# An audio tower on one core: how normalised tokens, projections and residual sums are handed between VectorE and TensorE around the attention

## The reference, cut to what matters

```
h = x[:, None, :]                                  # 64 sequences of 4000 samples
for w, g, b, s in convs:                           # seven convolutions, 128 channels
    h = gelu(layernorm(conv1d(h, w, s), g, b))     # layernorm over the channels
h = layernorm(h, fln_g, fln_b) @ proj_w + proj_b   # 64 x 12 tokens of 192
h = h + landmark_attention(layernorm(h))           # 12 heads of 16, pseudo-inverse in 6 rounds
h = h + experts(layernorm(h))                      # 8 routed experts, one shared
```

## Time and profile before

| | |
|---|---|
| time, median of 3 runs | 875.67 us (874.26 to 878.14) |
| profiled execution: its time | 875.06 us |
| profiled execution: span from first to last instruction | 873.3 us |
| busy, TensorE's matmuls | 757.3 us, 87% of the span |
| busy, VectorE | 624.9 us, 72% |
| busy, ScalarE | 329.4 us, 38% |
| busy, GpSimd | 314.7 us, 36% |

### The profile page before, as it was taken

How to read it: one execution, slowest core, us unless ns; L and a number is a source line. 1 busy time by engine, 2 the same in 40 slices (tenths; PEclk the granted TensorE clock), 3 DMA queues, 4 the chain that set the end, 5 groups by cost and what they waited for, 6 DMA issues and landing times. The chain is left out here.

```text
span 873.3 us, 11965 instructions
## 1 busy us (share of the span) xinstructions
PE 757.3 (87%) x4308; PEld 578.2 (66%) x4308; DVE 624.9 (72%) x1373; ACT 329.4 (38%) x562; POOL 314.7 (36%) x365
## 2 busy tenths in 40 slices
PE   0099999999998999999899898787888887899997
PEld 0055565656565655665565678677888886899977
DVE  7965778786788675456556568998888888462387
ACT  0054473436643565453332124022333321245433
POOL 1332313133133123212000037457777885247301
PEclk9997987998899989997898899899999999989999
DMA  2430520024000600000000430000000000200000
GB/s 74 85 88 1 102 53 1 1 47 106 1 1 12 130 1 1 1 1 0 1 1 2 171 165 1 1 1 1 1 1 1 1 2 0 82 1 1 1 1 28
DMA packets 23424, 25.50 MB, mean 29 GB/s; under 512 B 17370, under 2 KB 21530, under 8 KB 22442
## 3 DMA queue, kind: packets, MB, share of 16 engines
q1 hardware_dynamic: 23096, 24.17, 11.1%
q10 hardware_dynamic: 270, 0.58, 0.3%
HBM read 21.05 MB, written 3.66 MB: 28 GB/s over the span
## 5 line engine op out<-in xcount | busy, mean ns | idle before, releaser
L521 POOL TENSOR_TENSOR diff<-h 128x400 f32<-128x400 f32 x112 | 98.4, 901 | 280.1 <-ACT h L661 169.2
L607 PEld LDWEIGHTS ps<-averager,sq 128*100 128x100 f32 (+2 forms) x1024 | 105.3, 174 | 35.6 <-ACT sq L656 20.2
L607 PE MATMUL ps<-averager,sq 128*100 128x1 f32 (+2 forms) x1024 | 102.6, 227 | 9.6 <-ACT sq L656 9.4
L567 PE MATMUL ps<-h,w 128*128 128x400 f32 x224 | 108.1, 610 | 1.9 <-ACT h L635 1.1
L760 DVE TENSOR_TENSOR h<-ps,shared 128x800 f32<-128x800 f32 x56 | 55.4, 989 | 65.5 <-PE ps L576 65.5
L656 ACT ACTIVATE sq<-h 128x800 f32<-128x800 f32 (+1 forms) x58 | 50.1, 864 | 118.2 <-DVE h L760 111.0
L1103 PE MATMUL pt<-for_pe,ident 128*128 128x156 f32 (+2 forms) x420 | 70.1, 328 | 24.8 <-DVE for_pe L1302 24.8
L576 PE MATMUL ps<-diff,w 128*128 128x400 f32 x224 | 91.5, 530 | 0.0
L795 DVE TENSOR_TENSOR h<-h,ps 128x400 f32<-128x400 f32 (+1 forms) x116 | 61.5, 560 | 33.4 <-PE ps L626 33.0
L1103 PEld LDWEIGHTS pt<-for_pe,ident 128*128 128x128 f32 x420 | 63.7, 204 | 30.1 <-DVE for_pe L1302 27.7
L635 ACT ACTIVATE h<-ps,lnp 128x800 f32<-128x800 f32 x64 | 63.7, 1013 | 39.5 <-PE ps L540 39.4
(11 more groups left out here) (302 smaller groups left out, 1357.5 us busy)
## 6 DMA issues: line engine op xcount, KB each, us to landing
late<-windows_dram SPq DMA_DIRECT2D x18, 375.0 KB, 8.1
gate_w<-in_gate_w SPq DMA_DIRECT2D x1, 3456.0 KB, 11.5
up_w<-in_up_w SPq DMA_DIRECT2D x1, 3456.0 KB, 19.0
windows_dram<-parts SPq DMA_DIRECT2D x9, 250.0 KB, 5.5
acts<-in_down_w SPq DMA_DIRECT2D x1, 1728.0 KB, 9.0
late<-windows_dram SPq DMA_DIRECT2D x18, 93.8 KB, 4.8
w<-in_w SPq DMA_DIRECT2D x1, 1024.0 KB, 6.0
xs<-in_x SPq DMA_DIRECT2D x4, 252.5 KB, 3.7
```

Source lines behind the costliest of these rows:

```text
L521: pool.tensor_tensor(to[:, rows, :], here[:, rows, :], behind[:, rows, :], ALU.subtract).then_inc(diff_ready, 1)
L567: pe.matmul(out[:, c, :, :], w[:, L.first_tap + 1, :], plane(l, s, p, 1, slice(c, L.pos, 2)), start=True, stop=False)
L607: mm = pe.matmul(var_ps[0:L.w, at:at + 1], sq[:, square_of[r, l, s, p // 2] % 2, p % 2, q * L.w:(q + 1) * L.w], averager[:, 0:1], start=Tr ...
```

## The change

`normalise` writes the variance plus EPS where the copy put it, so the copy is gone (in all three uses). With a semaphore given, each normalised tile adds one to it, and TensorE's transposes wait tile by tile (`tokens_normed`, `x_normed`); the two telling copies are gone. Scale and offset are applied in two instructions, four tiles (one PSUM bank) and two, as soon as those are turned, and the projection waits for each part. The two projections tell after each pair of tiles (`tiles_projected`), and the additions behind them wait pair by pair. The blocks of `stay_warm` keep their lengths and places.

```
@@ normalise: EPS goes straight into stats, the copy goes, tiles are told one by one @@
-def normalise(nc, steps, src, dst, stats, mv, y, t, u):
+def normalise(nc, steps, src, dst, stats, mv, y, t, u, normed=None):
...
-    steps.done(nc.vector.tensor_scalar(mv[:, :, 1], mv[:, :, 1], EPS, None, ALU.add))
-    steps.settle()
-
-    steps.done(nc.vector.tensor_copy(stats[:, :, 0], mv[:, :, 1]))
+    steps.done(nc.vector.tensor_scalar(stats[:, :, 0], mv[:, :, 1], EPS, None, ALU.add))
     steps.settle()
     rsqrt(nc, steps, stats[:, :, 0], y, t, u)
     for i in range(TT):
-        steps.done(nc.vector.tensor_scalar(dst[i], src[i], mv[:, i, 0:1], y[:, i:i + 1], ALU.subtract, ALU.mult))
+        tile = nc.vector.tensor_scalar(dst[i], src[i], mv[:, i, 0:1], y[:, i:i + 1], ALU.subtract, ALU.mult)
+        if normed is None:
+            steps.done(tile)
+        else:
+            tile.then_inc(normed, 1)
     steps.settle()
 
 
-def turn(pe, ps, src, ident, done):
+def turn(pe, ps, src, ident, done, normed):
 
     for k in range(KD):
         for t in range(TT):
+            pe.wait_ge(normed, t + 1)
             mm = pe.transpose(ps[0:96, k, t * P:(t + 1) * P], src[:, t, 96 * k:96 * k + 96], ident[:, :])
         mm.then_inc(done, 1)
...
@@ attention, TensorE @@
                 stay_warm(bank(3, 1), 14)
-                pe.wait_ge(to_pe, 1)
                 for t in range(TT):
-                    mm = pe.transpose(pt[:, 1, t * P:(t + 1) * P], norm6[:, t, :], ident[:, :])
-                mm.then_inc(turned, 1)
+                    pe.wait_ge(tokens_normed, t + 1)
+                    pe.transpose(pt[:, 1, t * P:(t + 1) * P], norm6[:, t, :], ident[:, :]).then_inc(tokens_turned, 1)
                 stay_warm(bank(3, 1), 4)
-                pe.wait_ge(to_pe, 2)
                 pe.wait_ge(a_in, 16 * LOADS)
                 for t in range(TT):
+                    pe.wait_ge(to_pe, 1 + (t >= FIRST_TILES))
                     mm = pe.matmul(pt[:, 2 + t // 4, (t % 4 // 2) * 512 + (t % 2) * D:(t % 4 // 2) * 512 + (t % 2) * D + D],
                                    norm6t[:, t * P:(t + 1) * P], proj_w[:, :], start=True, stop=True)
-                mm.then_inc(projected, 1)
+                    if t % 2:
+                        mm.then_inc(tiles_projected, 1)
                 stay_warm(bank(3, 1), 26)
+                turn(pe, pt, xhat, ident, half_turned, x_normed)
+                stay_warm(bank(3, 1), 4)
                 pe.wait_ge(to_pe, 3)
-                turn(pe, pt, xhat, ident, half_turned)
-                stay_warm(bank(3, 1), 4)
-                pe.wait_ge(to_pe, 4)
                 pe.wait_ge(half_copied, 1)
...
@@ attention, VectorE @@
-                normalise(nc, steps, [pt[:, 0, t * P:(t + 1) * P] for t in range(TT)], tile(norm6), *small)
-                nc.vector.tensor_copy(t6[:, :], y6[:, :]).then_inc(to_pe, 1)
-                dve.wait_ge(turned, 2)
-                nc.vector.tensor_scalar(norm6t[:, :], pt[:, 1, 0:TOK], lnp[:, 14:15], lnp[:, 15:16],
-                                        ALU.mult, ALU.add).then_inc(to_pe, 1)
-                dve.wait_ge(projected, 1)
+                normalise(nc, steps, [pt[:, 0, t * P:(t + 1) * P] for t in range(TT)], tile(norm6), *small, tokens_normed)
+                for first, end in ((0, FIRST_TILES), (FIRST_TILES, TT)):
+                    dve.wait_ge(tokens_turned, end)
+                    nc.vector.tensor_scalar(norm6t[:, first * P:end * P], pt[:, 1, first * P:end * P], lnp[:, 14:15], lnp[:, 15:16],
+                                            ALU.mult, ALU.add).then_inc(to_pe, 1)
                 dve.wait_ge(a_in, 16 * LOADS)
...
-                for out, bank in projected_tiles():
+                for c, (out, bank) in enumerate(projected_tiles()):
+                    dve.wait_ge(tiles_projected, c + 1)
                     steps.done(nc.vector.tensor_tensor(out, bank, proj_b[:, :].unsqueeze(1).broadcast_to([P, 2, D]), ALU.add))
                 steps.settle()
-                normalise(nc, steps, tile(hidden), tile(xhat), *small)
-                nc.vector.tensor_copy(t6[:, :], y6[:, :]).then_inc(to_pe, 1)
+                normalise(nc, steps, tile(hidden), tile(xhat), *small, x_normed)
                 dve.wait_ge(half_turned, 1)
...
-                dve.wait_ge(projected, 2)
-                for out, bank in projected_tiles():
+                for c, (out, bank) in enumerate(projected_tiles()):
+                    dve.wait_ge(tiles_projected, TT // 2 + c + 1)
                     steps.done(nc.vector.tensor_tensor(out, out, bank, ALU.add))
```

More of the change, by code:

```diff
@@ L83 @@
 PADS = LANDMARKS - SEQ
+FIRST_TILES = 512 // P
 PINV_ITERS = 6
@@ L899, in attention @@
     to_pe = sem("to_pe")
-    projected = sem("projected")
+    tokens_normed = sem("tokens_normed")
+    tokens_turned = sem("tokens_turned")
+    tiles_projected = sem("tiles_projected")
+    x_normed = sem("x_normed")
     qkv_ready = sem("qkv_ready")
@@ L1128, in _ @@
                 stay_warm(bank(3, 1), 5)
-                pe.wait_ge(to_pe, 5)
+                pe.wait_ge(to_pe, 4)
                 pe.wait_ge(heads_ready, 2)
@@ L1260, in _ @@
                 copies(applying, at_applying)
-                act.wait_ge(turned, 3)
+                act.wait_ge(turned, 2)
                 for half in range(2):
@@ L1411, in _ @@
                                         attn[:, :, :].rearrange("p i (h d) -> p i h d", d=DH), ALU.subtract).then_inc(out_lanes, 1)
-                dve.wait_ge(turned, 3)
+                dve.wait_ge(turned, 2)
                 steps.done(nc.vector.tensor_copy(*heads_turned(1, 0)))
                 nc.vector.tensor_copy(*heads_turned(1, 1)).then_inc(to_pe, 1)
-                dve.wait_ge(projected, 2)
-                for out, bank in projected_tiles():
+                for c, (out, bank) in enumerate(projected_tiles()):
+                    dve.wait_ge(tiles_projected, TT // 2 + c + 1)
                     steps.done(nc.vector.tensor_tensor(out, out, bank, ALU.add))
```

## The result

| | before | after |
|---|---|---|
| time, median of 9 runs | 876.23 us (871.83 to 880.56) | 870.73 us (867.46 to 873.62) |
| ratio of the runs, 95% interval | | 0.9938 (0.9913 to 0.9963) |
| profiled execution, span | 873.3 us | 869.6 us |

The change takes 0.6% off, 5.4 us of 876 by the ratio, with 3.2 to 7.6 us inside the interval. The forecast was 869.8 us (867.2 to 872.6).

What follows compares the result with a forecast made beforehand. The bound was taken to be the back-and-forth chain between TensorE and VectorE. Terms 3.16 + 1.07 + 0.93 + 0.75 = 5.91 us took 875.06 to 869.15 us; 0.61 us for the median gave 869.8 us (867.2 to 872.6).

Steps and rivals of the forecast that it cites:

- The chain: Attention's opening: TensorE and VectorE wait on each other in turn; the edits start q, k and v 3.16 us earlier.
- Short steps: Copy dropped in each `normalise`: 0.20 us each for the first two; the third, before the experts, hidden by TensorE's `stay_warm`.
- Tokens turned by tile: Opening: first projection starts 1.27 us earlier, including the first 0.20 us short step; bounds 0.9 and 1.8 us.
- Bias and residual additions: Behind both projections: with additions by pairs, two of three are hidden, saving 0.93 us at each place.
- `turn`: Second six transposes, tile by tile: ScalarE's copy begins 1.05 instead of 1.81 us after VectorE's last tile, saving 0.76 us.
- the cover: The `stay_warm` block of 52 records behind the first projection: ends 0.7 us before VectorE's last tile, taken as enough slack.
- Clock behind `turn`: At the first q, k, v tile: TensorE's fall to 1.2 GHz goes with the wait, saving 1.07 us; other bound nothing.
- slower: Rival, chance 0.04: the 52-record `stay_warm` block runs at 1.2 GHz and becomes the bound; 878.8 us.
- Clock at the experts' start: Experts' `stay_warm` block: without the fall to 1.2 GHz VectorE is the bound, saving 0.75 us; bounds 0 and 0.75.
- Clock terms absent: Rival, chance 0.26: TensorE's clock still falls, behind another gap or before q, k, v; 4.09 us saved, 871.6 us.
- A fall less elsewhere: Rival, chance 0.12: one clock fall fewer in the iteration, worth at most 1.68 us; 868.1 us.
- Tiles bring nothing: Rival, chance 0.06: covers or per-tile waits hold TensorE; only short steps and last additions' pairs count, 1.7 us; 874.0 us.

Runs made afterwards that it cites:

- e1_short_step: Kernel before with only the variance-plus-EPS copy removed in all three uses of `normalise`; first `stay_warm` block to q, k, v 21.35 us, 0.43 less.
- e8_further: Changed kernel plus statistics begun after four turned tiles, scale and offset in three instructions, shorter `stay_warm` before the projection; 867.59 us, ratio to kernel before 0.9940.
- e3_pairs: Kernel before with only projections telling and additions waiting by pairs of tiles; first `stay_warm` block to q, k, v 20.83 us, output projection to experts 5.27 us.
- e4_turn: Kernel before with only the second `normalise` and `turn` going tile by tile; first `stay_warm` block to q, k, v 21.01 us, 0.77 less.
- e9_long_block: Changed kernel with 32 instead of 26 `stay_warm` matmuls behind the first projection; first `stay_warm` block to q, k, v 19.29 us, 0.91 more.
- e2_tokens: Kernel before with only tokens turned tile by tile and scale and offset in two instructions; first `stay_warm` block to q, k, v 20.45 us, 1.33 less.
- e5: Kernel before with 35 instead of 26 `stay_warm` matmuls, filling the wait before `turn`; first `stay_warm` block to q, k, v 21.75 us, first tile 2.21 us.
- e7: Changed kernel with 27 more semaphore increments on matmuls that nobody waits for; q, k, v products 11.88 us, output projection 4.14 us, as without them.
- before_again: Kernel before, unchanged, profiled a second time; first `stay_warm` block to q, k, v 22.92 us, `turn` itself 2.63 us instead of 1.52.
- before_third: Kernel before, unchanged, profiled a third time; first `stay_warm` block to q, k, v 21.76 us, no clock fall behind `turn`, experts' block 5.60 us.

## Why the prediction was right

**The chain.** The view that carried the forecast, a chain going back and forth with each engine waiting for all six tiles, is borne out by the parts alone: 3.48 us as a sum of four, 3.40 together, 3.16 forecast.

**Short steps.** 0.20 us each: 0.43 for two (e1_short_step).

**Tokens turned by tile.** Forecast 1.27 us with the step, measured 1.40 (8.46 to 7.06 us after the block's start), inside its bounds. In the timeline of the changed kernel the projection follows the block of 8 records without idle time. With 2 records, and scale and offset in three instructions, e8_further starts it 0.96 us earlier, of which 0.44 is the earlier start of VectorE; how the other two edits share the rest was not tried apart. The split of one instruction in two cost 0.17 us (1.25 against 1.08), where the prediction had 0.81 + 0.54 = 1.35 us for the two, and it is hidden.

**Bias and residual additions.** 0.93 us each: 0.95 and 0.93 measured alone (e3_pairs), 0.93 and 0.93 in the change.

**`turn`.** Forecast 0.76, measured 0.75 and alone 0.77 (e4_turn). The slack that I gave the cover, 0.7 us, was too large. The block does end 0.71 us before VectorE's last tile (510.72 and 511.43), but behind the block twelve transposes must run and behind the tile only seven: ScalarE's copy starts 1.34 us after the one at the earliest and 1.06 us after the other. That leaves 0.43 us (e9_long_block). It held, so the sum did not show it.

**Clock behind `turn`.** Forecast 1.07 us, measured 0.79 in the profiled pair. The size was off because I set the first tile against the next (1.94 us), while the first takes 2.22 us at full clock. More important, the term was taken from one execution as if the fall were part of the kernel. Behind a wait of 2.1 us it came in two of four executions (three of the kernel before and e2_tokens), behind 1.90 us not in the one (e1_short_step), behind waits of at most 1.2 us in none of eight (both of the changed kernel, e3, e4, e5, e7, e8, e9), behind 3.11 us in the one that had it. So the change removes a chance of a fall here, by the counts of four and eight, but a median had only about half of it to lose. The Trainium skill (TensorE: Matmul & The Clock Gate, What's actually happening) says that the chip watches TensorE in windows that do not start with the kernel. The different outcomes behind equal waits agree with it.

Two readings in this part of the prediction were wrong. It says that products behind a wait of 2.06 us took 3.71 us once and 5.39 us another time; the trace before has six such waits in the iteration, and five of the products took 3.71 us. One fall behind six such waits should have made the fall at `turn` a matter of chance in the sum. And against the rival *slower* it says that the clock was 1.2 GHz only after the wait at `turn`; it was so in the first block of `stay_warm` too (0.50, above).

**Clock at the experts' start.** Forecast 0.75, measured 0.63 to the first product. Behind 2.06 us the block took 7.0 to 7.2 us in four executions and 5.60 in three; behind 1.1 us it took 5.60 in all seven. The case without a fall in the kernel before has 10.49 us to the first product, so 0.44 us of the 0.63 is the fall and 0.19 the third short step. The prediction calls that step hidden by the block, and yet its 752.8 us for VectorE contains it (753.94 - 0.93 - 0.20). It is hidden only where a fall lengthens the block. By the prediction's own times the term would be 0.8 and not 0.75 (754.65 - 0.93 - 752.9).

**Sum.** The part that does not hang on the clock is 3.40 + 0.93 + 0.19 = 4.5 us. A fall at `turn` cost 0.79 in the first execution and 1.15 in before_again (22.92 against 21.77), half the time, say 0.5; one at the experts' start 0.44, in four of seven, 0.25. An estimate for the median is thus 5.3 us, against 5.4 measured (a ratio of 0.9938) and 5.91 forecast. By it the forecast sum was 0.6 us too high: the chain 0.24 too low, and the clock's two terms, with the third short step in the second, 0.9 too high (1.07 + 0.75 against 0.5 + 0.25 + 0.19), mostly because chances were counted as certain. The interval of the measurement, 3.2 to 7.6 us, could not have told.

The traces allow a check of this estimate that leaves out the tower. From the attention's first block to the end the three executions of the kernel before take 381.4, 380.0 and 376.3 us, the two of the changed kernel 373.9 and 373.9: 5.3 us by the means, but 2.4 to 7.5 by the pair that is taken. And the 5.3 is made up otherwise than in the sum. From the output projection to the end they take 132.1, 132.0 and 129.6 us before and 130.5 and 130.5 after, 0.7 us by the means, where the sum has 0.93 + 0.19 + 0.25 = 1.37; the fall behind the router's products, which the changed kernel has in both profiles, takes part of it back. Falls in the iteration, one more in the first execution, make up for that. That forecast, estimate and measurement lie so near together is luck in part.

**The rivals.** *Clock terms absent* (4.09 us) lies inside the interval, so the time does not exclude it, and before_third, one of three executions of the kernel before, has no fall to lose at either place. Its mechanism, a fall behind another gap, came true in part. At the two places the clock stayed at 1.00 in both profiles of the changed kernel, but behind the router's products it fell in both, where before_third has no fall: 2.1 us (114.9 against 112.9), more than the 0.44 that the experts' block gains. *A fall less elsewhere* happened in the profiled pair (iteration -1.77 us) and was made up for by the tower (+3.83 us). *Tiles bring nothing* and *slower* are excluded by the stretches.

What stays open: why the tower differs by up to ten microseconds between executions. Falls of the clock within it are the likely reason, by the granted clock of 0.91 to 0.89 and TensorE's 9.1 us more of busy time, but no run isolates them, and what decides whether a wait brings a fall is not shown. The clock's two terms are read from profiles; no difference in the time of whole executions shows them by themselves.

## What to carry to other kernels

Where two engines hand a whole array back and forth, price each hand-over from the timeline as "last piece done to next engine's start", and let pieces follow one another: here four such edits were worth 3.4 us, added up within 0.1 us, and could be forecast to a few tenths from rows of before. After each, look for the filler or the instruction that is late next, and measure its slack with everything that must pass behind it. A fall of the clock seen in one profile is a chance, not a term: profile the kernel before two or three times before its price goes into a sum, and compare stretches rather than whole times where the rest of the kernel varies by more than the change is worth.

## What the runs showed of the hardware that I had not expected

- At the two places that the change touches, a wait of TensorE of 2.1 us brought a fall to 1.2 GHz in six of eleven cases (two of four at `turn`, four of seven at the experts' start), waits of 1.2 us or less in none of fifteen.
- Elsewhere in the same kernel it is otherwise: 8 of 84 behind 2.06 us in the iteration, none of thirteen behind 2.55 us in front of the heads' transposes, fourteen of fourteen at the attention's first block, behind 1.45 us. In eleven of fourteen executions the mean granted clock in the 20 us behind the experts' first product is below 1.00, with falls behind small products that follow one another without a wait; it cost 0.6 to 2.1 us in the seven with the additions by pairs.
- A fall can hit the work at once (before_again, `turn` at 2.63 us) or come only behind it (the first profile, q, k and v); it cost 1.15 and 0.79 us.
- 27 semaphore increments more on two streams of float32 products cost 0.00 us.
- One program's conv tower, the same instructions each time, took 489.6 to 500.0 us in the profiled executions here.
